# Mamba-2 mixer and mixture of experts on one NeuronCore: the mixer's instructions in a new, finer order, and the weights of three experts loaded at another place

## What is computed

```python
x = x + mixer(_layernorm(x))      # Mamba-2 block with its own gated MLP
x = x + moe(_layernorm(x))        # top 2 of 8 experts

# mixer, on h = rmsnorm(x) * norm1_w
z, xBC, dt = split(h @ in_proj_w)                     # 512, 768, 8 columns
xBC = silu(causal_conv4(xBC));  xs, Bm, Cm = split(xBC)
y = ssd(xs, softplus(dt + dt_bias), -exp(A_log), Bm, Cm)   # chunks of 128 tokens, 8 heads
y = rmsnorm((y + D * xs) * silu(z)) * mixer_norm_w
h1 = res + y @ out_proj_w;  h2 = rmsnorm(h1) * norm2_w
out = h1 + (silu(h2 @ gate_w) * (h2 @ up_w)) @ down_w      # inner width 704

# experts: softmax router, two of 8, width 896, tokens sorted by expert
h = silu(ragged_dot(x_sorted, w1)) * ragged_dot(x_sorted, w3)
out = sum over the two choices of weight * ragged_dot(h, w2)
```

## Time and profile before

| | us |
|---|---|
| median of 3 runs (850.6 to 851.73) | 850.96 |
| the profiled execution | 855.37 |
| its span, first to last instruction | 853.6 |
| PE / DVE / ACT / POOL busy in it | 726.9 / 585.7 / 225.9 / 285.5 |
| mean granted TensorE clock | 0.921 of full speed |

### The profile page before, as it was taken

One profiled execution on the slowest core, in us unless ns is written; L12 is line 12 of the kernel. 1 busy time (PEld: TensorE's weight loads), 2 busy tenths in 40 slices (PEclk: granted clock), 3 DMA queues, 4 the chain that ended last, 5 costly groups with the idle time before them and its releaser, 6 DMA issues.

```text
span 853.6 us, 9996 instructions
## 1 busy us (share of the span) xinstructions
PE 726.9 (85%) x2695; PEld 468.5 (55%) x2696; DVE 585.7 (69%) x1457; ACT 225.9 (26%) x470; POOL 285.5 (33%) x475
## 2 busy tenths in 40 slices
PE   6768768998899869598820899999999999999992
PEld 4445455567556756374520466666666666666662
DVE  4968568667764754253460488888888888888880
ACT  1645354435343624124010111111111111111110
POOL 2122422233222342513431233443343343344322
PEclk9969969998999889799955899999999999999997
DMA  9202003000400034006687721121121111112111
GB/s 322 102 2 99 0 1 99 1 0 1 145 4 1 1 131 177 0 26 155 146 133 161 266 50 25 25 32 29 25 31 31 25 27 34 25 25 37 25 13 18
DMA packets 32669, 52.26 MB, mean 61 GB/s; under 512 B 4419, under 2 KB 24323, under 8 KB 32624
## 3 DMA queue, kind: packets, MB, share of 16 engines
q1 hardware_dynamic: 24096, 41.60, 16.9%
q0 software_dynamic: 8544, 10.30, 7.4%
HBM read 42.23 MB, written 9.81 MB: 61 GB/s over the span
## 4 chain that ended last, share of the span: by engine, by line
PE 64%; DVE 11%; issue 9%; DMA 6%; POOL 5%; ACT 3%; SPq 1%; DVEq 0%; POOLq 0%; ACTq 0%
PE ps L930 26%; PE ps L943 13%; DVE big L1384 3%; PE ps L682 3%; PE ps L691 3%; PE ps L705 3%; PE ps L405 3%; PE ps L458 3%; PE ps L525 2%; DMA big<-in_w 2%; PE ps L582 2%; DMA xn_rows<-big 2%; PE ps L472 2%; DVE big L1803 1%; PE ps L539 1%
## 5 line engine op out<-in xcount | busy, mean ns | idle before, releaser
L1803 DVE STREAM_TRANSPOSE big<-big 32x224 f32<-32x224 f32 x608 | 244.8, 403 | 9.1
L930 PE MATMUL ps<-big 128*128 x624 | 243.3, 543 | 1.1 <-ACT big L1293 1.1
L930 PEld LDWEIGHTS ps<-big 128*128 128x128 f32 x624 | 119.3, 192 | 106.4 <-issue 104.5
L943 PE MATMUL ps<-big 128*128 x546 | 124.5, 380 | 2.0 <-DVE big L1823 1.3
L1846 POOL TENSOR_TENSOR big<-big 128x1 f32<-128x1 f32 x153 | 48.5, 317 | 203.1 <-DVE big L1811 161.6
L943 PEld LDWEIGHTS ps<-big 128*128 128x128 f32 x546 | 100.8, 190 | 14.9 <-issue 2.9
L405 PE MATMUL ps<-big 128*128 128x128 f32 (+1 forms) x327 | 57.4, 291 | 49.0 <-DMA big<-lists,big 24.8
L1299 ACT ACTIVATE big<-ps 128x896 f32<-128x896 f32 x39 | 35.8, 917 | 217.8 <-PE ps L930 217.8
L405 PEld LDWEIGHTS ps<-big 128*128 128x128 f32 (+1 forms) x327 | 43.9, 153 | 82.6 <-issue 40.2
L1818 DVE TENSOR_TENSOR big<-big,ps 128x896 f32<-128x896 f32 x39 | 42.4, 1088 | 50.5 <-PE ps L930 50.4
L2008 POOL DMA_INDIRECT out_rows<-big x39 | 62.9, 1614 | 23.2 <-issue 23.2
(11 more groups left out here) (174 smaller groups left out, 910.7 us busy)
## 6 DMA issues: line engine op xcount, KB each, us to landing
big<-in_w SPq DMA_DIRECT2D x24, 896.0 KB, 10.2
big<-cum_rows SPq DMA_DIRECT2D x16, 512.0 KB, 5.5
out_rows<-big SPq DMA_DIRECT2D x4, 512.0 KB, 3.0
xn_rows<-big SPq DMA_DIRECT2D x4, 512.0 KB, 5.8
big<-in_hidden SPq DMA_DIRECT2D x1, 1536.0 KB, 11.9
big<-in_in_proj SPq DMA_DIRECT2D x1, 1288.0 KB, 6.9
big<-in_gate SPq DMA_DIRECT2D x1, 640.0 KB, 12.9
big<-in_up SPq DMA_DIRECT2D x1, 640.0 KB, 8.7
```

What stands on the lines that cost most here:

```text
L930: last = mm(bank(bk + n)[:, 0:HALF], xT[:, k, :], expert_cols(e, off + k * M + n * HALF, HALF), start=(k == 0), stop=(k == KD - 1))
L943: last = mm(bank(7)[:, 0:D], hTs[:, half, j * P:(j + 1) * P], expert_cols(e, 2 * KD * M + j * D, D), start=(j == 0), stop=(j == MB - 1))
L1803: last = V.transpose(hTs[c * SQ:(c + 1) * SQ, half, :].rearrange("p (j t) -> p j t", j=MB)[:, :, q * SQ:(q + 1) * SQ], ha[q * SQ:(q + 1) * ...
```

## The change

First, the weights: of experts 2 to 5 only expert 2 is still issued ahead of the last two stores. Experts 3 to 5 are issued behind the load of `rec0`, and 6 and 7 behind them as before. `ln1_stats(1)` takes the wait for the rest of the input with it, `dt_` takes the one for the weights of the projection.

```diff
--- before.py
+++ after.py
@@ -376,8 +376,7 @@
 
             sp.wait_ge(o_taken, SEQS * CH)
             sp.wait_ge(ssy_ready, SEQS * CH)
-            for e in range(EARLY, SOON):
-                load_next(e)
+            load_next(EARLY)
             store_x1(3)
             store_xn(3)
 
...
@@ -388,6 +387,8 @@
 
             sp.wait_ge(rec_out, 16 * CH * TOP * SEQS)
             sp.dma_start(rec0, lists[0:P, :]).then_inc(rec0_in, 16)
+            for e in range(EARLY + 1, SOON):
+                load_next(e)
 
             for half in range(2):
                 sp.wait_ge(xg_in[half], 16)
...
@@ -420,6 +421,8 @@
 
             def dt_(n):
 
+                if n == 0:
+                    pe.wait_ge(win_in, 16)
                 pe.wait_ge(hT0_taken, n + 1)
                 pe.wait_ge(hT1_taken, n + 1)
                 if n == 1:
...
@@ -659,7 +662,7 @@
                                   start=(k == 0), stop=(k == KD - 1))
                 last.then_inc(lg_ps, 1)
 
-            def mlp_up(n, j):
...
@@ -681,6 +684,9 @@
                 for k in range(KD):
                     last = mm(bank(gate_bank(n, j)), wgate[:, k, j * P:(j + 1) * P], h2T[:, k, :], start=(k == 0), stop=(k == KD - 1))
                 last.then_inc(gate_ps, 1)
+
+            def mlp_up(n, j):
+
                 if j > 0:
                     pe.wait_ge(gate_taken, nth(n, JB, j - 1))
                 elif n < SEQS - 2:
```

```diff
@@ -715,192 +721,251 @@
             pe.wait_ge(small_in, 32)
             keep_warm(MISC, WARM_START)
             hT_(0)
-            pe.wait_ge(win_in, 16)
             dt_(0)
             xbc_(0, 0)
             xbc_(0, 1)
+            xbc_(0, 2)
+            z_(0, 0)
             dec_(0)
-            for t in range(CH):
-                xbc_(0, t + 2)
-                z_(0, t)
+            xbc_(0, 3)
+            xbc_(0, 4)
+            xbc_(0, 5)
+            z_(0, 1)
+            z_(0, 2)
+            z_(0, 3)
             bg_(0)
             front(0, 0)
             hT_(1)
+            front(0, 1)
+            state_(0, 0)
             dt_(1)
-
-            front(0, 1)
             xbc_(1, 0)
-            dec_(1)
             xbc_(1, 1)
+
             diag(0, 0)
-            state_(0, 0)
             xbc_(1, 2)
-
             off_(0, 1)
-            diag(0, 1)
             state_(0, 1)
             xbc_(1, 3)
+            dec_(1)
+
+            diag(0, 1)
             front(0, 2)
             xbc_(1, 4)
             yT_(0, 0)
             xbc_(1, 5)
+            z_(1, 0)
+            z_(1, 1)
```

```diff
             mlp_down(2, 3)
-            positions(1)
+            out_(3, 3)
             keep_warm(DIAG, WARM_LAST)
             h2T_(3)
+            positions(1)
             xnT_(2, 0)
+            mlp_gate(3, 0)
             mlp_up(3, 0)
+            mlp_gate(3, 1)
+            mlp_up(3, 1)
             logits(2, 0)
             xnT_(2, 1)
-            mlp_up(3, 1)
+            mlp_gate(3, 2)
             logits(2, 1)
-            for j in range(2, JB - 1):
-                mlp_up(3, j)
+            mlp_up(3, 2)
+            mlp_gate(3, 3)
+            mlp_up(3, 3)
+            mlp_gate(3, 4)
+            mlp_up(3, 4)
+            mlp_gate(3, 5)
+            mlp_down(3, 0)
+            mlp_down(3, 1)
+            mlp_down(3, 2)
             positions(2)
-            mlp_up(3, JB - 1)
-            for t in range(CH):
-                mlp_down(3, t)
             turn_half(0)
+            mlp_down(3, 3)
             half_logits(0)
             turn_half(1)
             half_logits(1)
-            for n, ts in HALVES:
-                positions(n, ts)
-
+            positions(3, HALVES[0][1])
+            positions(4, HALVES[1][1])
 
```

ScalarE's waits, and a piece of its list (chunks 2 and 3 of sequence 1 and the start of 2):

```diff
@@ -1000,7 +1065,7 @@
                 act.wait_ge(dec_ps, n + 1)
                 if n > 0:
                     act.wait_ge(cum_out, 16 * n)
-                    act.wait_ge(apart_ready, n * CH)
+                    act.wait_ge(apart_ready, n * CH * 2)
                 A(cumT[0:CH * HEADS, :], bank(MISC)[0:CH * HEADS, M_CUM:M_CUM + P], ACT.Copy).then_inc(cumT_taken, 1)
                 A(cums.rearrange("p a b -> p (a b)"), bank(MISC)[:, M_DT + CH * HEADS:M_DT + 2 * CH * HEADS], ACT.Copy).then_inc(cums_taken, 1)
                 A(dec[n % 2].rearrange("p a b c -> p (a b c)"), bank(MISC)[:, M_DT:M_DT + 3 * CH * HEADS], ACT.Exp).then_inc(dec_taken, 1)
...
@@ -1017,7 +1082,7 @@
                 A(xc[n % 2][:, j, :], xc[n % 2][:, j, :], ACT.Silu).then_inc(xc_ready, 1)
 
             def decay(n, c):
-                act.wait_ge(apart_ready, nth(n, CH, c))
+                act.wait_ge(apart_ready, 2 * nth(n, CH, c))
                 A(em[n % 2][:, c, :], em[n % 2][:, c, :], ACT.Exp).then_inc(decays, 1)
 
             def front(n, c):
...
@@ -1062,6 +1127,9 @@
 
             def square_y(n, c):
                 act.wait_ge(y4_ready, nth(n, CH, c))
+                if n + c > 0:
+
+                    act.wait_ge(ssy_ready, n * CH + c)
                 A(junk_y, yb[:, c % 2, :], ACT.Square, accum_out=ssy[:, c:c + 1]).then_inc(ssy_ready, 1)
 
             def square_h(n, c):
```

```diff
-            both(2)
+            square_h(0, 1)
+            tap(2, 3)
+            square_h(0, 2)
+            square_h(0, 3)
+            tap(2, 4)
+            tap(2, 5)
+            z_silu(2, 0)
+            dec_e(2)
+            h2T0(0)
+            z_silu(2, 1)
...
+            z_silu(2, 2)
+            z_silu(2, 3)
+            yT_copy(1, 1)
+            gate(0, 0)
+            conv_silu(2, 2)
+            conv_silu(2, 3)
+            square_y(1, 1)
+            conv_silu(2, 4)
+            conv_silu(2, 5)
+            gate(0, 1)
+            decay(2, 0)
+            x_D(1, 2)
+
+            front(1, 3)
+            decay(2, 1)
+            gate(0, 2)
+            x_D(1, 3)
+            gate(0, 3)
```

VectorE's pieces and the head of its list:

```diff
@@ -1327,6 +1437,8 @@
             tab = Steps(v, table_step, 11)
 
             def ln1_stats(n):
+                if n == 1:
+                    v.wait_ge(x_rest, 16)
                 ln1.start(n)
                 for t in range(CH):
                     last = V.bn_stats(st6[:, t, :], x[:, n * CH + t, :])
...
@@ -1394,12 +1506,12 @@
             def over_head(a, n=HD):
                 return a.unsqueeze(2).to_broadcast([P, HEADS, n])
 
-            def apart(n, c):
+            def apart(n, c, part):
 
 
                 v.wait_ge(cums_taken, n + 1)
                 v.wait_ge(cum_in[c], 16 * (n + 1))
-                for hh in range(HEADS):
+                for hh in range(part * HEADS // 2, (part + 1) * HEADS // 2):
                     q = slice(hh * P, (hh + 1) * P)
                     last = V.tensor_scalar(em[n % 2][:, c, q], em[n % 2][:, c, q], cums[:, c, hh:hh + 1], 0.0, ALU.subtract, ALU.min)
                 last.then_inc(apart_ready, 1)
...
                 pick(rp, p1, o1, rm1, ts, steps)
 
+            def route_next(n, ts=ALL, seq=None, steps=rt_):
                 steps.then(V.scalar_tensor_tensor(rq[:, ts, :], o1[:, ts, :], -2.0, rp[:, ts, :], ALU.mult, ALU.add))
                 pick(rq, p2, o2, rm2, ts, steps)
                 V.tensor_tensor(sel[:, ts, :], o1[:, ts, :], o2[:, ts, :], ALU.add).then_inc(sel_ready, 1)
+
+            def route_rec(n, ts=ALL, seq=None, steps=rt_):
+                seq = n if seq is None else seq
                 steps.then(V.tensor_tensor(ps12[:, ts], p1[:, ts], p2[:, ts], ALU.add))
                 steps.then(V.reciprocal(pr12[:, ts], ps12[:, ts]))
                 for k, p in enumerate((p1, p2)):
```

```diff
@@ -1573,200 +1688,254 @@
             v.wait_ge(aneg_ready, 1)
             ln1_h(0)
             hT1(0)
+            ln1_stats(1)
             dt_abs_(0)
             dt_softplus(0)
             conv_taps(0, 0)
             conv_taps(0, 1)
             conv_taps(0, 2)
-            v.wait_ge(x_rest, 16)
-            ln1_stats(1)
             conv_taps(0, 3)
-            apart(0, 0)
             conv_taps(0, 4)
             conv_taps(0, 5)
+            apart(0, 0, 0)
             ln1_h(1)
+            apart(0, 0, 1)
             masked_G(0)
+            ln1_stats(2)
+            hT1(1)
             scores(0, 0)
-            apart(0, 1)
-            hT1(1)
+            apart(0, 1, 0)
+            apart(0, 1, 1)
+            apart(0, 2, 0)
+            apart(0, 2, 1)
+            scores(0, 1)
+            apart(0, 3, 0)
+            state(0, 0)
+            conv_taps(1, 0)
             dt_abs_(1)
-            apart(0, 2)
-            scores(0, 1)
+            apart(0, 3, 1)
+            off(0, 1)
             dt_softplus(1)
-            apart(0, 3)
-
-            conv_taps(1, 0)
+
             y_(0, 0)
-            state(0, 0)
+            conv_taps(1, 1)
+            conv_taps(1, 2)
```

GpSimd's scatter and the end of its list:

```diff
@@ -1911,14 +2080,12 @@
                 g.wait_ge(ln2_var, n + 1)
                 G.tensor_tensor(rs2[:, ts], ve2[:, ts], half[:, ts], ALU.pow).then_inc(ln2_r, 1)
 
-            def scatter(n, ts=ALL, seq=None):
-                seq = n if seq is None else seq
+            def scatter(n, t, seq):
```

(198 more changed lines are left out.)

683 lines of the change are left out of this document (342 added, 341 removed).

## The result

The changed kernel takes 792.93 us, median of 4 runs (791.72 to 796.12); the kernel before, run beside it, 851.35 us. The ratio is 0.9314, 95% interval 0.9279 to 0.9349. The forecast was 791 us. A second series gave 793.24 us (6 runs, ratio 0.9273, interval 0.9241 to 0.9304). The profiled execution took 792.77 us; its span is 790.9 us.

What follows compares the result with a forecast made beforehand. TensorE sets the pace, with some 98 us of mixer waits and clock surcharge, then the wait chain to the tiles. 13 + 5 + 10 + 15 + 17 = 60 us takes 855.4 to 795.4, less 4.4 gives 791; range 767 to 826.

Steps and rivals of the forecast that it cites:

- The start: Mixer's first stage, 121.4 us: reordered lists remove the wait of `dec_(1)`, `front(1, 1)` at 108; gain 13 (4 to 18).
- Middle stages and end of the mixer: Fewer TensorE waits, no scatter ahead of `plus_x_D`: gains 5 (0 to 9), 10 (0 to 16) and 15 (8 to 25).
- Somewhat over half: Share of TensorE's waits and surcharge in the two middle mixer stages taken as gained: 5 and 10 us.
- The estimate of the surcharge: Mixer time lost to the lower clock behind waits: 9.6, 3.0, 7.6 and 8.7 us in the four stages.
- From the last `mlp_down` to tile 0: Way from mixer to tiles, 49.9 us: stores no longer behind weights, sum 33; gain 17 (10 to 18).
- The rule on queues: DMA engines alternate between queues by packets, so a gather skips waiting for a whole load; by it the added 1.3 us were about 0.
- Rival 3: Way to the tiles: the 12.97 us landing is the scatters' own, so it gives only 7; 801 us, chance 0.08.
- Rivals 1: Whole kernel: waits only move, only the scatter and the way to the tiles gain; gain 27.5, 823 us, chance 0.20.
- rival 2: The order fits: nearly all waits and surcharge of the mixer's last three stages go; 767 us, chance 0.16.
- rival 5: TensorE's work breaks into pieces and stays at the lower clock; with 90 us of work 84 lost, 875 us, chance 0.04.
- Rival 4: Tiles: expert weights come too late for tile 7, 36 to 37 us lost; 827 us, chance 0.05.
- Table loads: ScalarE in the mixer: 26 table loads instead of 16, 1.28 us each, hidden; without cover 13 us in all.

Runs made afterwards that it cites:

- `weights_alone`: The kernel before with only experts 3 to 5 moved behind the load of `rec0`: 850.07 us, ratio 0.9958.

## Why the prediction was right, point by point

The time was met (791 forecast, 792.93 measured) with the right kinds of cause, but its closeness is luck. Two terms were off in opposite directions: the mixer gave 54.6 us where 43 were forecast, the way to tile 0 gave 8.4 where 17 were. The last step of the sum was chance too: it took 4.4 us off because the one profile before lay that far above its median, while the changed kernel's profile lay 0.2 us under its own. Profile against profile, 60 us were forecast and 62.6 measured.

- **The start: forecast 13, measured 20.5.** The direction was right, the size too small and beyond its own range of 4 to 18. `front(1, 1)` came at 100.93, ahead even of the 104 that the walk through the lists gave; I had added 4 us for waits that did not come. VectorE was busy for 82% of it (69% before), where the forecast had it nearly continuous. `dt_abs_(0)` came 2.5 us later, as foreseen (some 2).
- **Middle stages and end of the mixer: forecast 5 + 10 + 15 = 30, measured 34.1.** The first middle stage, forecast at 5, shows 1.0 by its marks; with the work that moved into it that says little. VectorE rose from 72% to 85% in it as foreseen; TensorE waited for it once for 1.86 us. `turn_half(0)`, put at minus 1.7, made TensorE wait for nothing. Shown one by one: `scatter(0)` (11.5 us in the old order, 7.6 in the new one, where the forecast had 12.2) and the gates apart from the ups (9.8 us at the end of the mixer, 7.3 against the second profile). "Somewhat over half" held: in the whole mixer 39 of 69 us of waits went. The estimate of the surcharge was too high: by it 28.9 us fell to 6, but TensorE's busy time fell by 15.7 only.
- **From the last `mlp_down` to tile 0: forecast 33, measured 41.4.** This is the step that failed, and it is mis-sized in one place above all. The last issue came 21.8 us after `mlp_down` (forecast 22.5; "now 25.7" is the end of that issue, its start is 24.8). The landing, put at 2.5 us, measured 9.6, from 389.43 to `rec0` at 399.00: 4.4 for a scatter by itself and about 5 of backlog. The 2.5 lie even below the gather's 2.7 that the same sentence names as the lower bound, when the earlier trace rows had the same operation at 13.9; of those, `weights_alone` leaves 8.7. `rec0` to tile 0, "6.7 plus 1.3", measured 10.0, since the gather took 6.05 us beside expert 3.
- **The rule on queues.** The gather took 2.95 us alone and 6.2 beside a 2,688 KB load on SP's queue. The Trainium skill ("DMA: Bandwidth & Descriptors", section on queues, rings and completion order) has the engines take turns by packets; the trace agrees in that the gather did not wait for the whole load, which takes some 10 us. But the extra 3.2 us were more than the 1.3 that I had added for it, so the load beside it is not free.
- **Rival 3**, that the 12.97 us are the scatters' own, was in the main right as a mechanism: 8.7 of 13.9 stay without weights. It did not set the time, because the mixer gave more.
- **Rivals 1, 2 and 5.** Few waits moved: the longest new one in the mixer is 2.46 us. The mixer's 54.6 us lie between the forecast's 43 and rival 2's 66. The clock rose to 0.97 to 1.00 in the mixer, which speaks against rival 5.
- **Rival 4.** The weights were in time: five loads at a pitch of 10.4 us from 399.37 on, the fifth issued at 440.79, and the tiles keep their pace. The prediction misread here: its second and third line are tiles 2 and 3, not 3 and 4. So tile 7 comes 19.6 + 5 x 9.26 = 65.9 us after tile 0, not 56.7, and rival 4 would have cost 28 us, not 36 to 37. Measured are 66.1, from 409.04 to:

```profile
475.14 6.18 PE L995 MATMUL ps<-big 128*128 x16
```

- **Table loads** rose from 16 to 26, at 1.28 us each, and stayed hidden: ScalarE is busy for 235.5 instead of 225.9 us, and TensorE waits for it nowhere above 0.7 us. No drain shows behind them, as the prediction had read: `decay(0, 0)` starts at 44.97, the table load ahead of it at 43.67.
- **What the prediction did not see:** that its two plain causes, the scatter and the weights, give 3.6 us each alone and 14.8 together. By subtraction the remaining 44 or so of the 58 us are the finer order; of its pieces only the gates were shown to matter (5 to 9 us), and what the others are worth is open.

## What to carry to other kernels

Where two chains end together, making one edit alone measures next to nothing (3.6 us each, 14.8 together); make both before the gain is judged, or undo each in the new kernel, where the same two were worth 8 to 12 and 3 to 7 us. A few large pieces (a gate block of TensorE, eight scatters of GpSimd) cut into single calls can be worth more as filler for short waits than the waits seem to cost, since the clock comes back too. Behind a burst of small transfers look for the time of a lone one before neighbours are blamed, and issue big loads behind the first short transfer on which everything waits, not beside it.

## What the runs showed of the hardware

- A single indirect scatter of 128 pairs of 8 bytes landed 4.4 us after its issue (one trace). The last of a burst, issued every 1.26 to 1.28 us, landed after 7.1 to 9.8 us, sooner the longer POOL had paused ahead of the last four, and beside weight loads after 13.7 to 14.0.
- An indirect gather of 128 rows was on TensorE 2.9 to 3.0 us after its issue with no load beside it (five traces), and 5.9 to 6.4 us beside a 2,688 KB weight load issued 2 us ahead of it (nine traces).
- The Trainium skill ("DMA: Bandwidth & Descriptors", section on the anatomy of a SWDGE transfer) gives about 2.0 us of fixed cost for a transfer issued from GpSimd; a lone scatter here took twice that (4.4 us).
- What the queue is slow at in such a burst (the descriptors, the writes to HBM or the signals) is open.
- The granted clock was 1.00 from `front(1, 1)` to `front(2, 1)` although TensorE waited 1.86 us once in it.
